# A gatv2 layer and a 64-expert layer in one kernel: message one-hots formed by VectorE, not turned by TensorE and copied by ScalarE

## What is computed

```python
# x [1250, 256], src and dst [40000], dst sorted
# graph layer, 4 heads of 64; W_l, W_r [256, 256]
xl, xr = LN(x) @ W_l, LN(x) @ W_r                 # [N, 4, 64]
e = leaky_relu(xl[src] + xr[dst], 0.2)            # [E, 4, 64]
score = einsum('ehd,hd->eh', e, att)
alpha = softmax of score over the edges with the same dst
agg = segment_sum(alpha * xl[src], dst)           # [N, 256]
x = x + LN(elu(agg + bias) + LN(x)) * gamma + beta
# expert layer: 64 experts, the top 2 of each of the 1250 tokens
x = x + sum over 2 experts of gate * (relu(LN(x) @ W1[e] + b1[e]) @ W2[e] + b2[e])
```

## Time and profile before

| | |
|---|---|
| median of 3 runs | 774.21 us (773.92 to 777.58) |
| span of the profiled execution | 870.6 us |
| PE busy | 721.0 us, 83% |
| DVE busy | 560.3 us, 64% |
| POOL busy | 411.5 us, 47% |
| ACT busy | 355.9 us, 41% |
| mean granted clock of TensorE | 0.913 |

### The profile page before, as it was taken

The page is one execution under the profiler, slowest core; times in us unless marked ns, Lnnn a source line. Parts: engine busy times, 40 slices in busy tenths (PEclk is TensorE's granted clock), DMA queues, the critical chain, the costliest instruction groups (busy, mean ns, idle before and its releaser), DMA issues. The chain is left out here.

```text
span 870.6 us, 14203 instructions
## 1 busy us (share of the span) xinstructions
PE 721.0 (83%) x4151; PEld 490.7 (56%) x4153; DVE 560.3 (64%) x1355; ACT 355.9 (41%) x1256; POOL 411.5 (47%) x405
## 2 busy tenths in 40 slices
PE   4844777997999889988988898998855499999995
PEld 2722444665666666666766565776544255555553
DVE  5653657886778777777876687878697333434333
ACT  1411334554455555555554464657632121121220
POOL 0566666366667656666765566710326011212121
PEclk9975798999999999999998899999955699999998
DMA  4545463344354435353534353510299899999995
GB/s 122 98 156 148 111 170 97 113 114 125 94 150 112 135 90 149 100 144 95 156 95 125 97 139 108 133 30 1 93 411 405 249 317 367 367 369 370 368 390 200
DMA packets 66875, 154.81 MB, mean 178 GB/s; under 512 B 17390, under 2 KB 30142, under 8 KB 66769
## 3 DMA queue, kind: packets, MB, share of 16 engines
q1 hardware_dynamic: 45824, 100.40, 34.2%
q0 software_dynamic: 18384, 51.06, 21.5%
q10 hardware_dynamic: 2592, 2.43, 0.9%
HBM read 138.76 MB, written 15.39 MB: 177 GB/s over the span
## 5 line engine op out<-in xcount | busy, mean ns | idle before, releaser
L131 POOL DMA_INDIRECT G<-xl_tab,srcI x324 | 344.6, 1064 | 196.0 <-issue 80.4
L783 ACT ACTIVATE L<-psE 128x264 f32<-128x264 f32 x324 | 126.4, 390 | 277.6 <-PE psE L696 200.0
L696 PE MATMUL psE<-G,ident 128*128 128x264 f32 x648 | 209.2, 406 | 0.0
L707 PE MATMUL agg<-msg,M 128*128 128x256 f32 x648 | 191.2, 395 | 6.4 <-issue 4.8
L693 PE MATMUL psE<-xr,MT 128*128 x972 | 176.9, 292 | 0.0
L854 DVE TENSOR_TENSOR L<-L,attb 128x792 f32<-128x792 f32 x108 | 105.7, 978 | 93.6 <-ACT M L784 46.5
L689 PE MATMUL psE<-identb,MT 128*128 128x128 bf16 x324 | 74.1, 229 | 81.4 <-issue 39.2
L805 ACT ACTIVATE msg<-G,A 128x64 f32<-128x64 f32 x432 | 136.8, 354 | 1.5 <-PE agg L707 1.2
L707 PEld LDWEIGHTS agg<-msg,M 128*128 128x128 f32 x648 | 118.5, 194 | 33.3 <-issue 17.4
L693 PEld LDWEIGHTS psE<-xr,MT 128*128 128x128 bf16 x972 | 88.5, 101 | 41.7 <-issue 6.0
L696 PEld LDWEIGHTS psE<-G,ident 128*128 128x128 f32 x648 | 105.5, 203 | 5.1
(11 more groups left out here) (302 smaller groups left out, 723.1 us busy)
## 6 DMA issues: line engine op xcount, KB each, us to landing
w<-in_L_ffn_W SPq DMA_DIRECT2D x120, 512.0 KB
relb<-rel_d SPq DMA_DIRECT2D x36, 288.0 KB
G<-xl_tab,srcI POOLq DMA_INDIRECT x324
tabs<-tab_d SPq DMA_DIRECT2D x48, 98.2 KB
X<-xs_d SPq DMA_DIRECT2D x58, 64.5 KB
xn<-in_L_ffn_W SPq DMA_DIRECT2D x6, 512.0 KB
h_in<-in_L_ffn_W SPq DMA_DIRECT2D x6, 512.0 KB
xs_d<-zslot SPq DMA_DIRECT2D x8, 322.5 KB
```

Of the source, the lines that this page charges most:

```text
L131: nc.gpsimd.indirect_dma_start(out=G[:, g % RG, u * DX:(u + 1) * DX], out_offset=None, in_=xl_tab, in_offset=bass.IndirectOffsetOnAxis(ap= ...
L696: nc.tensor.matmul(psE[:, e, 0:DX], ident[:, :], G[:, s % RG, u * DX:(u + 1) * DX], start=False, stop=True).then_inc(expanded, 1)
L707: last = nc.tensor.matmul(agg[:, bass.ds(w * D, D)], M[:, s % RM, u * P:(u + 1) * P], msg[:, s % RA, u * D:(u + 1) * D], start=False, stop ...
L783: nc.scalar.activation(L[s % RL][:, u * DX:(u + 1) * DX], psE[:, e, 0:DX], ACT.Relu)
```

## The change

M is no longer made from MT. DVE forms it by itself, by a comparison: `place(s)`, a TENSOR_TENSOR with `is_equal` over 128 partitions and 3 x 128 fp32 columns, writes 1 where the number of the column (`iota32`, repeated for the three items) equals the place of the partition's edge (`relc`, one column for an item, repeated along 128). It stands in DVE's program behind `build_onehot`, once a step. `relc` is new: [128, 324] fp32, made in `node_phase` from `relm` by three PE transposes into psI and one ACT activation with bias -1.

With it L689 goes from `expand`, L784 from `evacuate` with its waits for `agged` and `tab_out` (which `place` has now), and the cast to `identb` from `node_phase`. `consumed` is counted up by the last product with xr3 of the second item, not by L689. `weight` has one more wait, for `placed`. The matrix of zeros that clears `agg` is 128 columns repeated four times; some semaphores are merged.

```diff
@@ node_phase, ACT
+            act.wait_ge(rel_ps, 2)
+            nc.scalar.activation(relc[:, :], psI[:, 0:NI], ACT.Copy, bias=-1.0, scale=1.0).then_inc(xlr_sb, 1)
             act.wait_ge(c_in, 64)
+            act.wait_ge(xlr_sb, NW + 1)
@@ node_phase, PE, behind project(1, i)
+            pe.wait_ge(rel_set, 2)
+            for c in range(CH):
+                last = nc.tensor.transpose(psI[:, c * CI:(c + 1) * CI], relm[:, c, :], ident[0:CI, 0:CI])
+            last.then_inc(rel_ps, 1)
@@ node_phase, DVE
-            dve.wait_ge(consts, 2)
-            c(nc.vector.tensor_copy(identb[:, :], ident[:, :]))
@@ graph_phase, expand
-                turned = nc.tensor.matmul(psE[:, e, DX:DX + P], mt, identb[:, :], start=True, stop=True)
+                for j in range(3):
+                    last = nc.tensor.matmul(psE[:, e, 0:DX], mt, xr3[:, bass.ds(w * (3 * DX) + j * DX, DX)], start=(j == 0), stop=False)
                 if u == 1:
-                    turned.then_inc(consumed, 1)
-                for j in range(3):
-                    nc.tensor.matmul(psE[:, e, 0:DX], mt, xr3[:, bass.ds(w * (3 * DX) + j * DX, DX)], start=(j == 0), stop=False)
+                    last.then_inc(consumed, 1)
@@ graph_phase, evacuate
-                if u == 0 and s >= RM:
-                    act.wait_ge(agged, s - RM + 1)
-                if (s, u) == (RM - TS - LS, 0):
-                    act.wait_ge(tab_out, 16 * (NB + 1))
-                nc.scalar.activation(L[s % RL][:, u * DX:(u + 1) * DX], psE[:, e, 0:DX], ACT.Relu)
-                nc.scalar.copy(M[:, s % RM, u * P:(u + 1) * P], psE[:, e, DX:DX + P]).then_inc(evacuated, 1)
+                nc.scalar.activation(L[s % RL][:, u * DX:(u + 1) * DX], psE[:, e, 0:DX], ACT.Relu).then_inc(evacuated, 1)
@@ graph_phase, DVE
+            def place(s):
+                if s >= RM:
+                    dve.wait_ge(agged, s - RM + 1)
+                if s == RM - TS - LS:
+                    dve.wait_ge(tab_out, 16 * (NB + 1))
+                V.tensor_tensor(M[:, s % RM, :].rearrange("p (u n) -> p u n", u=U), iota32[:, :].unsqueeze(1).broadcast_to([P, U, P]),
+                                relc[:, s * U:(s + 1) * U].unsqueeze(2).broadcast_to([P, U, P]), ALU.is_equal).then_inc(placed, 1)
@@ graph_phase, weight
                 if k == 0:
                     dve.wait_ge(alpha_set, b + 1)
+                    dve.wait_ge(placed, GPB * (b + 1))
@@ graph_phase, DVE's loop, behind build_onehot
+                if s < STEPS:
+                    place(s)
```

More of the change, by code:

```diff
@@ L183, in gnn_moe @@
             attb = gsb("attb", [P, DX])
-            identb = gsb("identb", [P, P], BF16)
             srcI = gsb("srcI", [P, NI], I32)
+            relc = gsb("relc", [P, NI])
             G = gsb("G", [P, RG, U * DX])
@@ L228, in node_phase @@
 def node_phase(nc, v):
[L230 to L233, removed]
+    (x, src, dst, Wl, Wr, att, bias, gamma, beta, srcp, dstp, xl_tab, rel_d, ends_d, ident, prow, iota32,
+     xs, xn, xr3, attb, bg, srcI, relc, wrow, wblk, G, M, gathered, relb, rel_in, valid, gd, ends_out, zslot, zset) = (v[k] for k in (
+         "x src dst Wl Wr att bias gamma beta srcp dstp xl_tab rel_d ends_d ident prow iota32 "
+         "xs xn xr3 attb bg srcI relc wrow wblk G M gathered relb rel_in valid gd ends_out zslot zset").split())
     with ExitStack() as ctx:
@@ L293, in node_phase @@
         gd_set, srcI_set = sem("gd_set"), sem("srcI_set")
-        iotas, zeroed = sem("iotas"), sem("zeroed")
+        zeroed = sem("zeroed")
         rel16_set, rel_out = sem("rel16_set"), sem("rel_out")
@@ L397, in _ @@
         def _(pe):
-            pe.wait_ge(consts, 2)
+            pe.wait_ge(consts, 5)
             pe.wait_ge(before_set, 1)
@@ L521, in _ @@
             c.then(nc.vector.tensor_tensor(valid, clampd[:, :, :], dstF[:, :, :], ALU.is_equal))
-            c.then(nc.vector.scalar_tensor_tensor(out=relm[:, :, :], in0=dstF[:, :, :], scalar=1.0, in1=valid,
-                                                  op0=ALU.add, op1=ALU.mult))
+            nc.vector.scalar_tensor_tensor(out=relm[:, :, :], in0=dstF[:, :, :], scalar=1.0, in1=valid,
+                                           op0=ALU.add, op1=ALU.mult).then_inc(rel_set, 1)
+            dve.wait_ge(rel_set, 2)
             nc.vector.tensor_scalar(rel16[:, :, :], relm[:, :, :], -1.0, None, ALU.add).then_inc(rel16_set, 1)
@@ L540, in graph_phase @@
 def graph_phase(nc, v):
-    (xl_tab, rel_d, tab_d, ends_d, thr_d, ident, identb, prow, bg, xs, xn, xr3, attb, srcI, wrow, wblk, G, M, msg, gathered, relb, rel_in,
+    (xl_tab, rel_d, tab_d, ends_d, thr_d, ident, prow, bg, xs, xn, xr3, attb, srcI, wrow, wblk, G, M, msg, gathered, relb, rel_in, iota32, relc,
      marks, valid, gd, cut, ends_out, zslot, zset, zout, xs_d, agg) = (v[k] for k in (
-         "xl_tab rel_d tab_d ends_d thr_d ident identb prow bg xs xn xr3 attb srcI wrow wblk G M msg gathered relb rel_in "
+         "xl_tab rel_d tab_d ends_d thr_d ident prow bg xs xn xr3 attb srcI wrow wblk G M msg gathered relb rel_in iota32 relc "
          "marks valid gd cut ends_out zslot zset zout xs_d agg").split())
@@ L573, in graph_phase @@
         gcol = sb("gcol", [P, HEADS])
-        zero = sb("zero", [P, 512], BF16)
+        zero = sb("zero", [P, P], BF16)
         one = sb("one", [RB, P])
@@ L591, in graph_phase @@
         folded = sem("folded")
+        placed = sem("placed")
         block = ctx.enter_context(nc.Block())
@@ L746, in _ @@
                     if (s, u) == (1, 0):
-                        pe.wait_ge(init, 1)
+                        pe.wait_ge(marked, 3)
                         for j in range(NW * D // 512):
-                            nc.tensor.matmul(agg[:, j * 512:(j + 1) * 512], zero[:, 0:P], zero[:, :], start=True, stop=False,
-                                             skip_group_check=True)
+                            nc.tensor.matmul(agg[:, j * 512:(j + 1) * 512], zero[:, :], zero[:, :].unsqueeze(1).broadcast_to([P, 512 // P, P]),
+                                             start=True, stop=False, skip_group_check=True)
                     if 0 <= b < NB:
```

14 lines of the change are left out of this document (7 added, 7 removed).

## The result

The changed kernel takes 804.5 us (median of 4 runs, 801.18 to 804.84), the kernel before 775.89 us (median of 4, 773.92 to 778.24): a ratio of 1.0325, with an interval of 1.0279 to 1.0371. It is slower: the medians lie 28.6 us apart, and the ratio puts it at 25 us. The forecast was 791, 17 us slower than before, in a range of 757 to 811.

What follows compares the result with a forecast made beforehand. POOL's gathers, with PE right beside them, were taken to pace the loop. Loop +7.7 for DVE's work, +7 to +10 for waits, +0 to +3 for POOL out of step made +17: 774 to 791 us, range 757 to 811.

Steps and rivals of the forecast that it cites:

- The bound before: Graph loop: timed runs lack the profile's pauses, POOL's gathers set the pace, last gather at 481 us, loop 444.6 us.
- PE and ACT: Graph loop: L689 gone saves PE 17.8 us, L784 gone saves ACT 84.9 us, both lost in idle time.
- DVE's term: Graph loop: place adds 0.47 us each, 50.8 us in all, bringing DVE's work from 401.5 to 452.3 us.
- Even without one wait it is 7.7 us too long: Graph loop: DVE's 452.3 us of work exceeds the present loop of 444.6 us, so the loop must lengthen.
- POOL's term: Gathers starting under place are held: 0.29 hits a step of 0.22 us, 7 us in all, bounds 0 and 13.
- falling out of step: Graph loop: POOL, close to DVE's pace, costs 3 us more when the two fall out of step.
- The two rows agree: Two earlier gathers fit the port lock: 1.69 us when begun after an L854, 0.95 when begun ahead of an L872.
- The bound of 13 us: Upper bound of hold-up under place: the gathers' mean excess, 39 us, times 0.56 / 1.67 of the instructions' length.
- +7 to +10 for DVE: Graph loop: waits that DVE keeps at the start, for first gathers, edge tables and first evacuations, add +7 to +10 us.
- The remaining signs: Profile after: span 870.6 plus 5 to 20, DVE's steady waits 50 us or less, share over 0.8, gathers near 1.09 us.
- three signs of being wrong: DVE still waits 90 us and PE never for it; place well under 0.47 us; time changes elsewhere than the loop's end.
- Rival (c): Graph loop: DVE as bound breaks the softmax's round trips and granted clock falls, +25 to +30 on top, 815 us; chance 0.13.

Runs made afterwards that it cites:

- before, again: The kernel before, unchanged, run and profiled once more: 779.97 us, with a profiled span of 778.2 us.
- filler with one input: Changed kernel, but from step 22 a one-input instruction feeding nothing replaces place, one-hots stay stale: 788.51 us, ratio 1.0165 on chip D.
- place behind score: Changed kernel with place moved in DVE's program from behind build_onehot to behind score: 815.87 us, ratio 1.0494.
- changed kernel's second run: The changed kernel itself, unaltered, run and profiled again on another chip: 801.64 us, ratio 1.0326.
- compare with one input: Changed kernel with place comparing relc with the constant 5.0, one SBUF input: 3985.2 us, only its loop is read, last gather ends at 496.4.
- no place: Changed kernel with place working only for the first 22 steps, its one-hots then reused: 785.01 us, ratio 1.0093.
- two-input filler: Changed kernel, but from step 22 a two-input instruction feeding nothing replaces place: 855.87 us, ratio 0.9954, and 864.16 us, ratio 0.9882, on two chips.
- ACT weighing two: Changed kernel with weighing of the second item moved from DVE to ACT, DVE's weight cut to one item: 869.87 us, ratio 1.0076.

## Why the prediction came out as it did

**The bound before: confirmed.** The prediction took the 96.4 us between profile and median as pauses and put the last gather at 481 us without them. Before, again has them gone and the last gather at 490.7; the 9.7 us are the excess, 46.9 instead of the 38.5 that the profile with pauses showed, and 1.3 more. The loop, to the last score, took 450.0 us and not 444.6.

**PE and ACT: confirmed, and worth nothing.** Undisturbed items of PE are 1.21 us apart (timeline of PE after):

```profile
299.18 0.50 PE L697 MATMUL psE<-xr,MT 128*128 x3
...
300.39 0.50 PE L697 MATMUL psE<-xr,MT 128*128 x3
...
301.61 0.50 PE L697 MATMUL psE<-xr,MT 128*128 x3
```

The prediction said 1.215. ACT's busy time fell from 361.2 to 308.0 us, by 53 and not by 85: the copy's 0.26 us in its row overlap the next instruction by about 0.11 (on ACT's timeline of before, again the copy of 258.36 is followed at 258.50), so it held ACT for some 0.15 us, 48 us in all. That error cost nothing, since ACT waits.

**DVE's term: right in size, wrong in what it decides.** In the loop (50 us to the last score) DVE's waits are 54.4 us of 450.0 in before, again and 28.4 of 471.4 after. Its work is thus 395.6 and 443.0 us, so place took 47.4 us where the prediction had 50.8 and a total of 452.3. The step that failed is the one behind it, "Even without one wait it is 7.7 us too long": 443.0 would have fitted in the 450 of the loop before, with 7.0 to spare. Of the 14.7 us between the two, the loop's length makes 5.4, DVE's work before 5.9 and place 3.4. A margin of 7.7 us, less than 2% of the loop, had been taken from an execution with pauses. DVE is busier than any engine in the loop (437.2 of 471.4 us, 0.93), and still waits 28.4 us, while POOL waits 3.0 us. The engine that ended the loop was POOL before, and it is POOL after. The filler with one input puts nearly the same load on DVE (438.9 us of work) and takes 13 us less, and DVE waits for 20.0 us of its loop; with place behind score DVE's work is the same and its loop 12 us longer. A DVE that sets the pace would allow neither.

**POOL's term: the mechanism right, the size too small by a factor of three.** The prediction had 7 us, at most 13, and 3 for falling out of step; measured are 67.9 - 46.9 = 21.0 us. The mechanism is the one that it read from the earlier trace rows, and the runs show it: the second input alone adds 12 to 16 us to the gathers on three chips, and 13.1 us to the time where POOL has no slack. This is the exclusive lock that the Trainium skill (SBUF — State Buffer, "SBUF: two separate sides") describes for a VectorE operation with two SBUF inputs and a GpSimd one that reads SBUF, and the traces agree as far as the gather goes. That section also lets a GpSimd operation that started first block the other; here that wasn't seen (last section), and the measurement decides. The prediction's "The two rows agree" is therefore right of the first row alone: in the second the gather started first, and the L872 behind it took 0.69 us, as its mean.

What was mis-sized shows when the gathers are counted by the instruction of DVE under which each starts (a start up to 0.02 us ahead is counted in; where two instructions overlap, a few gathers could stand in either row, while the sums hardly move):

| starts under | before, again: count, mean hold, sum | after: count, mean hold, sum |
|---|---|---|
| attend's product (L854, L864) | 81, 0.374 us, 30.3 | 66, 0.510 us, 33.6 |
| weight (L872, L883) | 31, 0.284 us, 8.8 | 26, 0.098 us, 2.6 |
| place (L857) | none | 35, 0.464 us, 16.3 |
| scans of the softmax (L898, L907) | 6, 0.494 us, 3.0 | 10, 1.14 us, 11.4 |

The number of hits came out, 35 for the 0.29 x 108 = 31 of the prediction, though "place behind" with its 103 shows that a count by chance can be far off. A hit was priced at 0.22 us and costs 0.464 on average. But the average hides two kinds. Three of the 35 start with place and are not held; 23 are held to place's end alone, 4.2 us in all. Nine are held on, although place has ended: five to the end of weight, which follows place without a gap and has two SBUF inputs too, and four through weight and the next attend as well. These nine cost 12.1 us. One held to place's end, of after:

```profile
285.36 0.54 DVE L857 TENSOR_TENSOR M<-iota,relc 128x384 f32<-128x384 f32 x1
285.66 1.06 POOL L131 DMA_INDIRECT G<-xl_tab,srcI  x1 [0.30 <-issue]
285.82 0.68 DVE L883 TENSOR_TENSOR msg<-G,A 128x512 f32<-128x512 f32 x1
```

One held on to weight's end, first DVE and then POOL:

```profile
289.70 0.55 DVE L857 TENSOR_TENSOR M<-iota,relc 128x384 f32<-128x384 f32 x1
290.17 0.68 DVE L883 TENSOR_TENSOR msg<-G,A 128x512 f32<-128x512 f32 x1
```

```profile
288.52 0.95 POOL L131 DMA_INDIRECT G<-xl_tab,srcI  x1 [0.30 <-issue]
289.77 1.90 POOL L131 DMA_INDIRECT G<-xl_tab,srcI  x1 [0.30 <-issue]
```

And one held through the attend behind them:

```profile
251.04 2.81 POOL L131 DMA_INDIRECT G<-xl_tab,srcI  x1 [0.30 <-issue]
```

The gather of 289.77 starts 0.07 us into place, which ends at 290.25. A gather that is held ends 0.82 us behind the end of what holds it (0.945 less the 0.125 that the hold falls short of what was left), which would be 291.07. It ends at 291.67, and that is 0.82 behind the end of weight, at 290.85. One hit, 0.95 us. Held to place's end only, the hits would have cost 7.3 us, the 7 of the prediction; what it left out are the holds that run on. All nine gathers start in the first 0.18 us of place, but others that do are held to its end only; what decides it, no run here shows.

Place's hits account for 16.3 of the 21.0 us, and for 13.7 of 21.7 in the changed kernel's second run. The rest are shifts: a DVE with less idle time brings its other instructions closer together. The clearest is the row of the scans, 3.0 us before and 11.4 after, and it comes with a one-input instruction as well: 11.7 us with the filler of chip D, 12.9 with the compare with one input. The bound of 13 us missed both: it scaled the old excess by length.

**The sum.** +7.7 and +7 to +10 for DVE fall away, and +21.0 for POOL stands in their place, together with up to 3 us behind the loop (250.3 against 247.1, and 247.7 in the changed kernel's second profile, so I take it as scatter). The remaining 4 us to the 28.6 between the medians are the kernel before itself, whose profiled execution took 779.97 us, 4.1 above its first median. The forecast of 791 had the right sign and the right stage, from a sum whose larger part, some 15 of its 17 us, named the wrong engine. That the measured time lies in the range is partly luck.

**Split of the cost.** By the excess, before, again to the changed kernel's second run (21.7 us): 1.9 from the removals and the 22 compares left in "no place", 6.7 from a one-input instruction of that length on DVE, 13.1 from the second input. The middle term is about the growth of the scans' row, from 4.0 us in "no place" to 11.7. The first two come from runs on two chips and are within a few us of each other's scatter; the last is from one chip.

**The remaining signs.** The span should have grown by less than the time, because the profile's pauses would stay; the profiled execution had none of them, so this can't be judged. DVE's waits below 50 us came out (28.4 in the whole loop), and its share above 0.8 too (0.93), but before, again has 0.87 already. The gather's mean was forecast at 1.09 us and is 1.154. None of the three signs of being wrong appeared: they would have caught a DVE with much idle time, and not one that is nearly full and still isn't the engine that ends the loop. Rival (c), broken round trips of the softmax, did not come either: DVE's waits for exp fell from 14.1 to 5.5 us, and PE waits 1.6 us for endc and csum.

**Open.** What makes the pauses on two of the chips. Whether the changed kernel costs anything there was not measured: the two-input filler costs nothing, and the changed kernel with ACT weighing two 0.8%. What lets some holds run on past the instruction under which the gather started. A compare whose column numbers lie in PSUM, with one SBUF input left was not tried. No version here beats the kernel before.

## What to carry to other kernels

When an engine's work moves to VectorE, look at what GpSimd does meanwhile: an instruction with two SBUF inputs lengthens a GpSimd gather that starts under it, and if GpSimd sets the pace, that is the price, not VectorE's own time. The end of that instruction is only the least that a hit costs: where the next one follows without a gap, some holds run on through it, so leave room in the upper bound. Test the cost with an instruction of the same length and one SBUF input. And before a sum is built on one profile whose span is far from the median, find out which engine has least idle time once the pauses are taken out, and keep that engine in every later step of the sum.

## What was not expected of the hardware

A gather can be held although it starts under an instruction that holds nothing. DVE and POOL at 308 us, after:

```profile
308.69 0.37 DVE L907 TENSOR_TENSOR_SCAN csum<-thr,psS 1x112 f32<-1x112 f32 x1
308.83 2.21 POOL L131 DMA_INDIRECT G<-xl_tab,srcI  x1 [0.30 <-issue]
308.99 0.35 DVE L909 TENSOR_TENSOR_SCAN csum<-thr,psS 1x112 f32<-1x112 f32 x1
309.27 0.95 DVE L864 TENSOR_TENSOR L<-L,attb 128x792 f32<-128x792 f32 x1
```

The gather ends at 311.04, again 0.82 us behind the end of attend's product at 310.22, although it began under a scan on a single partition, which reads one operand from SBUF and one from PSUM. It isn't the scans that hold it. In 34 cases of all the profiled executions a gather starts under such a scan and attend does not follow at once, and each of them takes 0.95 us or less. One of them, in after, where attend starts just as the second scan ends and not 0.07 us ahead:

```profile
136.00 0.37 DVE L907 TENSOR_TENSOR_SCAN cmax<-thr,psS 1x112 f32<-1x112 f32 x1
136.30 0.35 DVE L909 TENSOR_TENSOR_SCAN cmax<-thr,psS 1x112 f32<-1x112 f32 x1
136.64 0.98 DVE L864 TENSOR_TENSOR L<-L,attb 128x792 f32<-128x792 f32 x1
```

```profile
136.14 0.95 POOL L131 DMA_INDIRECT G<-xl_tab,srcI  x1 [0.30 <-issue]
```

So it looks as if attend held the gather, and already 0.44 us ahead of its own start, where it runs on from the instruction before. It doesn't do so every time: in "no place" the gather of 136.16 us takes 0.95, with the same distance to such an attend. On the other side, a gather begun just ahead of a place is not held at all, nor is the place: in after 50 gathers begin 0.02 to 0.06 us ahead of one and take 0.946 us on average, and these places 0.558. One of them:

```profile
307.58 0.95 POOL L131 DMA_INDIRECT G<-xl_tab,srcI  x1 [0.30 <-issue]
307.61 0.56 DVE L857 TENSOR_TENSOR M<-iota,relc 128x384 f32<-128x384 f32 x1
```

The chips differ by more than the change does: the same kernel before takes 775 to 779 us on some and 864 and 874 us on two others, in every one of their runs, with pauses that the profile calls "remote" (19.5 us of POOL's waits on chip B). A change that costs 3.3% on the first costs nothing on the others by the two-input filler, and 0.8% by the kernel with the lighter weight; the change itself was not run there.
